# Half-height matmuls two at once, PSUM banks leased by twos, and biased logits in SBUF, in a decoder layer

## What is computed

```python
x = _layernorm(x + _L0_attn_ref(x, ...))        # scores = LN(x) K^T, 1024 keys, relu, square, times V, per head of 64
x = _layernorm(x + _L0_xattn_ref(x, ctx, ...))  # 16 heads of 16; logits + stoich_bias, softmax, times V, Wo
x = _layernorm(x + _L0_ffn_ref(x, ...))         # 256 -> 1024 -> 256 with relu, low-rank part of the top-1 expert
...
        D = jnp.clip(frac[:, None, :] - frac[:, :, None], CLAMP_MIN, CLAMP_MAX)
        stoich_bias = ap * jnp.maximum(D, 0.0)[:, None] + an * jnp.minimum(D, 0.0)[:, None]
        attn = gamma * logits + delta * stoich_bias
        probs = jax.nn.softmax(attn, axis=-1)
```

## Time and profile before

| | |
|---|---|
| median of 3 runs | 865.58 us (864.62 to 867.97) |
| profiled execution, its own time | 868.24 us |
| span of its profile | 866.4 us |
| mean granted TensorE clock | 0.987 |
| busy PE / DVE / ACT / POOL | 824.3 / 720.1 / 704.0 / 581.2 us |

### The profile page before, as it was taken

The page is one execution under the profiler, slowest core; times in us unless marked ns, Lnnn a source line. Parts: engine busy times, 40 slices in busy tenths (PEclk is TensorE's granted clock), DMA queues, the critical chain, the costliest instruction groups (busy, mean ns, idle before and its releaser), DMA issues.

```text
span 866.4 us, 23427 instructions
## 1 busy us (share of the span) xinstructions
PE 824.3 (95%) x8444; PEld 594.3 (69%) x8444; DVE 720.1 (83%) x2148; ACT 704.0 (81%) x1930; POOL 581.2 (67%) x754
## 2 busy tenths in 40 slices
PE   7889899999999999999999999999999999999896
PEld 6545556767777676767767676676768667667686
DVE  5887988887888888888888888888888887889854
ACT  3658998897888989798897979888898988888841
POOL 5677878675777868586786768678776867543511
PEclk9998999999999999999999999999999999999899
DMA  7233222222131213223122312313231321323100
GB/s 170 99 65 69 50 56 44 42 40 56 44 62 44 56 38 57 45 52 67 44 57 44 68 26 60 59 45 61 50 63 20 64 55 32 62 45 56 32 14 25
DMA packets 38149, 46.32 MB, mean 53 GB/s; under 512 B 10417, under 2 KB 27313, under 8 KB 38034
## 3 DMA queue, kind: packets, MB, share of 16 engines
q1 hardware_dynamic: 38034, 44.82, 26.0%
HBM read 15.42 MB, written 4.19 MB: 23 GB/s over the span
## 4 chain that ended last, share of the span: by engine, by line
PE 84%; DVE 5%; ACT 4%; issue 2%; POOL 2%; SPq 1%; DMA 1%; POOLq 0%; DVEq 0%; ACTq 0%
PE bank L308 12%; PE bank L503 12%; PE bank L295 11%; PE bank L256 10%; PE bank L421 8%; PE bank L435 7%; PE bank L405 4%; PE bank L381 4%; PE bank L362 2%; PE bank L328 2%; PE bank L342 2%; PE bank L513 2%; PE bank L387 2%; ACT P L711 1%; DVE T L939 1%
## 5 line engine op out<-in xcount | busy, mean ns | idle before, releaser
L1165 POOL TENSOR_TENSOR R<-R 128x512 f32<-128x512 f32 x208 | 220.4, 1063 | 74.8 <-ACT R L655 74.4
L711 ACT ACTIVATE P<-T,NM 128x256 f32<-128x256 f32 x512 | 256.9, 512 | 13.0 <-DVE NM L939 12.9
L1183 POOL TENSOR_SCALAR U<-DP,alph 128x512 f32<-128x512 f32 x256 | 188.1, 736 | 108.5 <-DVE NM L939 72.8
L930 DVE SCALAR_TENSOR_TENSOR bank<-DN,alph,bank 128x512 f32<-128x512 f32 x256 | 180.2, 749 | 47.3 <-PE bank L405 47.1
L939 DVE CUSTOM_DVE_ANT_0 T<-bank,U 128x256 f32<-128x256 f32 x512 | 185.9, 419 | 2.4 <-POOL U L1183 1.3
L655 ACT ACTIVATE R<-bank 128x512 f32<-128x512 f32 x248 | 134.0, 597 | 30.9 <-PE bank L295 29.2
L633 ACT ACTIVATE STG<-bank 128x512 f32<-128x512 f32 x256 | 138.5, 596 | 13.9 <-PE bank L421 12.5
L308 PE MATMUL bank<-R,VS 128*32 128x512 f32 x992 | 120.6, 602 | 6.2 <-DVE R L884 3.8
L295 PE MATMUL bank<-SK,KH 64*128 64x512 f32 x480 | 107.4, 443 | 5.7 <-ACT XO L655 2.4
L711 ACT ACTIVATION_READ_ACCUMULATOR P<-T,NM 128x1 f32 x512 | 103.6, 202 | 0.0
L421 PEld LDWEIGHTS bank<-ident,P 64*128 64x128 f32 x2048 | 77.1, 140 | 36.4 <-issue 27.7
(11 more groups left out here) (180 smaller groups left out, 1826.2 us busy)
## 6 DMA issues: line engine op xcount, KB each, us to landing
QS<-QK SPq DMA_DIRECT2D x384, 64.0 KB, 2.3
XG<-in_x SPq DMA_DIRECT2D x16, 256.0 KB, 3.0
CT<-in_ctxT SPq DMA_DIRECT2D x16, 256.0 KB, 2.9
out<-XO SPq DMA_DIRECT2D x15, 256.0 KB, 2.5
FK<-in_frac SPq DMA_DIRECT2D x16, 128.0 KB, 3.2
STG<-in_wiT SPq DMA_DIRECT2D x2, 512.0 KB, 5.5
STG<-in_woT SPq DMA_DIRECT2D x2, 512.0 KB, 4.3
STG<-in_kT SPq DMA_DIRECT2D x2, 256.0 KB, 4.1
```

Of the source, the lines that this page charges most:

```text
L711: eng.activation(P[n % NP][:, cs], T[n % NT][:, cs], ACT.Exp, bias=NM[:, n % 8, q:q + 1], scale=-1.0, accum_out=SU[n // 16 % 2][:, q, seat ...
L930: eng.scalar_tensor_tensor(out=L[:, :], in0=dn[:, :], scalar=alph[:, 16 + h:17 + h], in1=L[:, :], op0=ALU.mult, op1=ALU.add).then_inc(s_t1, 1)
L1165: eng.tensor_tensor(r, r, r, ALU.mult).then_inc(s_sqp, 1)
L1183: eng.tensor_scalar(U[n % NU][:, :], dp[:, :], alph[:, h:h + 1], 0.0, ALU.mult, ALU.add).then_inc(s_u, 1)
```

## The change

- Every full-height product is cut into two half-height ones (rows 0 to 63 and 64 to 127). `products` issues them in pairs: in phase 0 the lower half of product `x` beside the upper half of product `y`, in phase 1 the halves crossed. The two go to different banks. Phase 1 waits on a semaphore (`s_half`) that the last matmul of phase 0 sets, since it adds to the same banks from the other rows. `kp` and `vp` are paired with each other, the others with their own second half. The transposes are cut in the same way, and the fillers too. Only `av`, `values` and one small product (`bias_o`) keep 128 rows. The count of matmuls in the program goes from 7342 to 10488.
- PSUM: six banks are three pairs, and every step leases a pair (`lease`), picked at build time by a table of expected durations. The logits lose their own two banks and lease a pair as well. `fo` and the two `fi` of a batch hold a pair each for long.
- `biased`: the first operation writes `T` in SBUF, not the bank, and waits for `T` to be free (`s_ex`); the second reads `T` and `U`, both in SBUF. A logits pair is free after the first operation (`s_t1`), and `logits` no longer waits for `s_tt`.
- `y1` becomes two operations on half the columns; other readers of transposed tiles read two banks with a strided pattern.
- All numbers of the order tables are new (a few are shown).

```diff
-        psum = [ctx.enter_context(nc.psum_tensor(f"bank{i}", [128, 512], f32)) for i in range(8)]
-        pL, pV, pA = psum[4:6], psum[6], psum[7]
+        turf = ctx.enter_context(nc.psum_tensor("turf", [128, 6, 512], f32))
+        psum = [turf[:, k, :] for k in range(6)]
+        pV, pA = (ctx.enter_context(nc.psum_tensor(n, [128, 512], f32)) for n in ("valued", "heads"))
...
+        def quads(ap):
+            return ap.rearrange("p (a j x) -> p a j x", j=2, x=64)
+
+        def both(name, b, i=0):
+            k = place[name, b, i]
+            return turf[:, k:k + 2, :]
+
+        def woven(name, b, rows=slice(0, 128), a=4):
+            return both(name, b)[rows, :, 0:64 * a].rearrange("p j (a x) -> p a j x", x=64)
+
+        moment, expected, tenant, bank_of, place = [0], [-99999] * 3, [None, None, None], {}, {}
+        LEASE = {"lg": 21, "turn": 28, "sc": 26, "fi": 86, "fo": 197, "kp": 65, "qp": 34, "op": 22, "gate": 25,
+                 "gsT": 2, "uT": 18, "xnT": 26, "otT": 40, "x1T": 18, "rcT": 23, "x2T": 12, "bo": 452}
...
-        def take(name, b, i=0, keep=False):
-            k = ring.pop(0)
-            if not keep:
-                ring.append(k)
-            before = used.get(k)
-            used[k] = (name, b, i)
-            bank_of[name, b, i] = psum[k]
-            return psum[k], before
-
-        def give_back(name, b, i=0):
-            ring.append([k for k in used if used[k] == (name, b, i)][0])
+        def lease(*names):
+            p = min(range(3), key=lambda q: (expected[q], q))
+            expected[p] = max(expected[p], moment[0]) + LEASE[names[0][0]]
+            before, tenant[p] = tenant[p], names
+            for j, n in enumerate(names):
+                bank_of[n], place[n] = psum[2 * p + j], 2 * p + j
...
+            def two(name, b, i=0):
+                banks, before = lease((name, b, i), (name, b, i + 1))
+                banks_free(before)
+                return banks
+
+            def products(x, y, terms, phase, fresh):
+                for n, (lx, rx, ly, ry) in enumerate(terms):
+                    eng.matmul(x, lx[half(phase), :], rx[half(phase), :], start=(fresh and n == 0), stop=False,
+                               skip_group_check=True)
+                    end = eng.matmul(y, ly[half(1 - phase), :], ry[half(1 - phase), :], start=(fresh and n == 0),
+                                     stop=False, skip_group_check=True)
+                return end
 
...
-                        i = eng.transpose(bank[:, hp * 256 + t * 128:hp * 256 + t * 128 + 128],
-                                          XN[:, t, hp * 128:hp * 128 + 128], ident[:, :])
+                        for j in range(2):
+                            o = hp * 128 + t * 64
+                            i = eng.transpose(banks[j][:, o:o + 64], XN[half(j), t, hp * 128:hp * 128 + 128],
+                                              ident[half(j), half(j)])
...
+            def kp_vp(b, phase):
+                if phase == 0:
+                    _, before = lease(("kp", b, 0), ("vp", b, 0))
+                    banks_free(before)
+                    pe.wait_ge(s_wlo["k"], 1)
+                    pe.wait_ge(s_wlo["v"], 1)
+                    pe.wait_ge(s_ch, b + 1)
+                    pe.wait_ge(s_cl, b + 1)
+                else:
+                    pe.wait_ge(s_half["kp"], b + 1)
+                x, y = bank_of["kp", b, 0], bank_of["vp", b, 0]
+                (kh, kl), (vh, vl) = W["k"], W["v"]
                 for m in range(2):
                     cs = slice(m * 128, m * 128 + 128)
+                    terms = []
                     for k in range(2):
+                        terms += [(kh[:, k, cs], CH[:, k, :], CH[:, k, cs], vh[:, k, :]),
+                                  (kl[:, k, cs], CH[:, k, :], CH[:, k, cs], vl[:, k, :]),
+                                  (kh[:, k, cs], CL[:, k, :], CL[:, k, cs], vh[:, k, :])]
+                    o = slice(m * 256, m * 256 + 256)
+                    end = products(x[:, o], y[:, o], terms, phase, phase + m == 0)
+                if phase == 0:
+                    end.then_inc(s_half["kp"], 1)
+                else:
+                    end.then_inc(s_kvp, 1)
...
             def logits(p):
                 G, m = p // 2, p % 2
                 pe.wait_ge(d_q[G % 2], 96 * (G // 2 + 1))
-                pe.wait_ge(s_tt, 4 * p)
+                pL = two("lg", 0, 2 * p)
...
+            def ffn_in(b, v):
+                u, phase = v // 2, v % 2
+                if phase == 0:
+                    two("fi", b, 2 * u)
+                    pe.wait_ge(s_wlo["i0"], 1)
+                    pe.wait_ge(s_wlo["i1"], 1)
+                    pe.wait_ge(s_x2l, b + 1)
                 else:
+                    pe.wait_ge(s_half["fi"], 2 * b + u + 1)
                 for i in range(2):
+                    x, y = (bank_of["fi", b, 2 * u + j][:, i * 256:i * 256 + 256] for j in range(2))
+                    cx, cy = (slice((4 * u + 2 * j + i) * 128, (4 * u + 2 * j + i) * 128 + 128) for j in range(2))
+                    terms = []
                     for k in range(2):
+                        for w, z in ((WI[0], X2H), (WI[0], X2L), (WI[1], X2H)):
+                            terms.append((w[:, k, cx], z[:, k, :], w[:, k, cy], z[:, k, :]))
+                    end = products(x, y, terms, phase, phase + i == 0)
+                if phase == 0:
+                    end.then_inc(s_half["fi"], 1)
+
+            def low_rank(b, v):
+                u, phase = v // 2, 1 - v % 2
...
+                if piece % 2:
+                    pe.wait_ge(s_half["fo"], 2 * b + piece // 2 + 1)
+                x, y = (bank_of["fo", b, j][:, 0:256] for j in range(2))
+                pe.wait_ge(s_il, 4 * b + piece // 2 * 2 + 2)
+                terms = []
+                for c in range(piece // 2 * 4, piece // 2 * 4 + 4):
+                    tx, ty = (slice((c % 2) * 256 + t * 128, (c % 2) * 256 + t * 128 + 128) for t in range(2))
+                    for h, w in ((IH, WP[0]), (IH, WP[1]), (IL, WP[0])):
+                        terms.append((h[:, c // 2, tx], w[:, c, :], h[:, c // 2, ty], w[:, c, :]))
+                end = products(x, y, terms, int(piece in (1, 2)), piece == 0)
+                if piece % 2 == 0:
+                    end.then_inc(s_half["fo"], 1)
+                elif piece == 3:
+                    end.then_inc(s_fo, 1)
 
...
-                for b, u in due(g, -11, 8, 74, early=35, late=5):
+                for b, u in due(g, 18, 8, 70, early=-27, late=-28):
                     logits(8 * b + u)
-                for b, u in due(g, 1309, 4, 29, early=-19, late=239):
+                for b, u in due(g, 1295, 4, 23, early=-3, late=528):
                     ffn_in(b, u)
-                for b, u in due(g, 1310, 4, 29, early=-16, late=370):
+                for b, u in due(g, 1340, 4, 12, late=531):
...
-                b3 = bank_of["otT", b, 0][:, :].rearrange("p (t c) -> p t c", t=2)
+                x4 = quads(xg[:, :, :].rearrange("p t c -> p (t c)"))
                 dve.wait_ge(s_otT, b + 1)
-                eng.scalar_tensor_tensor(out=xg[:, :, :], in0=xg[:, :, :], scalar=2.0, in1=b3, op0=ALU.mult,
-                                         op1=ALU.add).then_inc(s_y1, 1)
-                dve.wait_ge(s_y1, b + 1)
+                for j in range(2):
+                    b3 = bank_of["otT", b, j][:, 0:256].rearrange("p (a x) -> p a x", x=64)
+                    eng.scalar_tensor_tensor(out=x4[:, :, j, :], in0=x4[:, :, j, :], scalar=2.0, in1=b3, op0=ALU.mult,
+                                             op1=ALU.add).then_inc(s_y1, 1)
+                dve.wait_ge(s_y1, 2 * b + 2)
                 stats("b", b, xg)
 
...
-                    h, L = head(n), pL[n % 2]
-                    eng.scalar_tensor_tensor(out=L[:, :], in0=dn[:, :], scalar=alph[:, 16 + h:17 + h],
+                    h, t, L = head(n), T[n % NT], bank_of["lg", 0, n]
+                    dve.wait_ge(s_ex, 2 * (n - NT + 1))
+                    eng.scalar_tensor_tensor(out=t[:, :], in0=dn[:, :], scalar=alph[:, 16 + h:17 + h],
                                              in1=L[:, :], op0=ALU.mult, op1=ALU.add).then_inc(s_t1, 1)
                 for n in pair:
-                    u, t, L = U[n % NU], T[n % NT], pL[n % 2]
+                    u, t = U[n % NU], T[n % NT]
                     dve.wait_ge(s_t1, n + 1)
                     dve.wait_ge(s_u, n + 1)
-                    dve.wait_ge(s_ex, 2 * (n - NT + 1))
                     for q in range(2):
                         cs = slice(q * 256, q * 256 + 256)
-                        eng.tensor_tensor_reduce(out=t[:, cs], in0=L[:, cs], in1=u[:, cs], scale=-1.0, scalar=BIG,
+                        eng.tensor_tensor_reduce(out=t[:, cs], in0=t[:, cs], in1=u[:, cs], scale=-1.0, scalar=BIG,
                                                  op0=ALU.add, op1=ALU.min,
```

(13 more changed lines are left out.)

599 lines of the change are left out of this document (265 added, 334 removed).

## The result

The changed kernel takes 901.03 us (median of 4 runs, 899.67 to 902.93) where the kernel before takes 865.32 us (4 runs on the same chip): a ratio of 1.041, 95% interval 1.038 to 1.044. It is 35.7 us slower; 16.7 was forecast. The span of its profile is 901.1 us, against 866.4.

A forecast was written before the change was run, and what follows sets the result against it. TensorE (49.5 of 50.0 us a batch) bounds the kernel before; afterwards VectorE, at 51.2. The added 1.2 us over 14 batches is +17 on 868.24: 885, less 2.7 for the median: 882 us, range 836 to 920.

The forecast's parts named there:

- the lock: VectorE bursts with two SBUF inputs and GpSimd operations take turns on shared ports, overlapping about 0.1 us: 7.3 us a batch.
- VectorE as the bound: Middle batches: VectorE busy 49.4 us, 51.2 with waits for ScalarE, against TensorE's 47.5.
- The start and the end I leave as they are.: Kernel's first and last parts, some 70 us each: no change forecast; the added 1.2 us applied to 14 steady batches.
- The wait of the bursts: VectorE's eight bursts a batch: 7.3 us added by waiting for GpSimd; bounds 4.5 and about 10.
- 1.8 us a batch of waits for `IH`: VectorE waiting for ScalarE's answers: 28.6 us in all, taken to stay whatever the period is.
- TensorE's term: TensorE's matmuls and transposes: -51 - 10 + 5 + 1 + 15 = -40 us, 2.5 us a batch.
- a second phase behind its first: TensorE drains between phases at 52 places: 0.27 to 0.3 us each, +15 us in all.
- a change of shape: TensorE switching array rows and columns in use: about 0.20 us each, 254 fewer, -51 us.
- The faster rival: TensorE stays the bound and the change pays: 48.4 us a batch, 839 us; chance 0.31.
- The banks' rival: Three PSUM pairs stall TensorE: four places, 6 us a batch, 53.5 us a batch, 918 us; chance 0.13.
- L930's -1.0 us a batch: First operation of `biased` writing SBUF: 749 ns priced at L890's 687, 16 a batch.
- 911: Time in us if GpSimd's 9.41 us inside bursts count in full, 2.1 us a batch more.

The follow-up runs named there:

- small_gp: Changed kernel with GpSimd's `U` and squares writing 32 of 512 columns, part of the computation left out: 864.1 us, ratio 0.997.
- before_small: Kernel before with GpSimd's `U` and squares cut to 32 of 512 columns, part of the computation left out: 857.8 us, ratio 0.992.
- lg_in_bank: Changed kernel with `biased` writing back to the logits' bank, the burst reading it, and the pair leased to the burst's end: 957.8 us, ratio 1.106.
- before_sbuf: Kernel before with `biased` writing `T` in SBUF, the burst reading `T` and `U` there, and the free-`T` wait moved ahead: 929.0 us, ratio 1.073.
- whole_products: Changed kernel with full-height products, one bank per phase, and no `s_half` waits between phases: 927.6 us, ratio 1.071.
- small_gp_free: `small_gp` with UL's copies reading constants so nothing waits for `uT`'s pair, more of the computation left out: 864.5 us, ratio 0.996.
- lg_late: Changed kernel, burst still reading SBUF, but the logits' pair leased until the burst's end (`s_tt`): 1027.6 us, ratio 1.186.
- guard: Changed kernel with GpSimd waiting for a burst's end ahead of 53 of its 338 two-input operations: 897.7 us, ratio 1.034.

## Why the prediction was wrong in size

The side was right, and the lock is there. The rise is twice the forecast, and what the forecast made of the lock, VectorE as the bound, did not come. By the medians, the cut of GpSimd's two operations gives the kernel before 7.7 us (865.6 to 857.8) and the changed one 37.0 (901.0 to 864.1). The difference, **29 us, is what those two operations and the bursts lose to each other** (31 if each run is taken against the kernel before of its own chip). The other **6 us** (864.1 against 857.8) are what halves, leases and places cost in sum, together with XN's gain and bias, which the bursts of `small_gp` still meet. Nearly all of the 6 is in the first three batches: 137.2 us in `small_gp`, 130.5 in `before_small`. The split takes it that the cut acts on both kernels alike. That it gives 7.2 us to `lg_in_bank`, which has no lock and no full engine, speaks for this; it is no proof.

- **The step that failed: "The start and the end I leave as they are."** I put the lock on 14 steady batches, 1.2 us each, since the view I had read closely was that of the middle. Its 11 steady batches did take 1.25 us more each, 13.8 in all. But the stretches that I had left at nothing gave 20.9 us of the 34.7, the first three batches 15.5 of them. `before_sbuf`, which has nothing of the change but the SBUF inputs, shows the start's share by itself: its first three batches take 149.4 us, at a mean clock of 0.97, against 135.5 before and 151.0 after. `small_gp` brings them to 137.2. The lower clock adds to the start of the changed kernel; by the distances of `whole_products` it is some 5 of the 15.5 us there, an estimate (TensorE is busy at the lower level for 21.4 us of this stretch after, for 9.5 before). First `before_sbuf`, then `small_gp`, then `before_small`:

```profile
62.70:212.10 149.40, 126.88 (x1324) 82.67 (x1325) 133.82 (x357) 121.04 (x343) 116.12 (x132) 0.97 0.24 46
57.70:194.90 137.20, 123.17 (x1680) 82.58 (x1682) 115.00 (x360) 120.39 (x344) 60.90 (x130) 0.95 0.28 53
57.40:187.90 130.50, 123.25 (x1336) 82.08 (x1335) 109.70 (x359) 121.00 (x346) 51.25 (x131) 1.00 0.28 53
```

- **The wait of the bursts was sized at 7.3 us a batch; it is 3.5** (55.6 us over 16), below my lower bound of 4.5. I counted every microsecond of GpSimd inside a burst as one in which the burst can't run. Most of it is `U`, which the burst's own second operation releases, and which then waits itself: 963 ns on average for the first head's `U`, 723 for the second's. Of the bursts' 55.6 us `U` caused 0.6, squares 29.0 and XN's two operations 21.1.
- **VectorE as the bound, 49.4 us busy and 51.2 with its waits, fell.** It is busy for 46.3 of 51.5. The 1.8 us a batch of waits for `IH`, which I had taken to stay whatever the period is, went from 28.6 to 10.7 us in all. That the period came out within 0.3 us is no credit to the sum: its errors met. No engine is full, and the chain passes through all four, 43, 25, 14 and 6%.
- **TensorE's term was too large.** 2.5 us a batch were to be saved; it is 1.5 (546.1 to 529.4 over eleven), and a batch has TensorE busy for 48.0 us where 49.5 less 2.5 would be 47.0. The 256-column pair starts every 0.12 us, the full one's price, as forecast. But the entry cost is not gone: the first pair after transposes still takes 0.08 us more (385.69, 385.89, then 386.02), where I forecast nothing. And a second phase behind its first costs 0.34 us, not 0.27 to 0.3: from the last pair of the first phase to the second pair of the second it is 0.57 us where two steps of 0.12 would do. The 0.26 us of the waits above (13.3 us for 52) is only what the load of the weights waited. With 0.34 and 0.12 in the sum, both this saving and the shapes' 1.6 us a batch of `whole_products` come to 0.13 to 0.14 us for a change of shape, an estimate, where I had 0.20.

```profile
385.69 0.36 PE L277 MATMUL turf<-Woh,CH 64*128 64x256 f32 x1
385.89 0.28 PE L277 MATMUL turf<-Wol,CH 64*128 64x256 f32 x1
386.02 0.28 PE L277 MATMUL turf<-Woh,CL 64*128 64x256 f32 x1
...
386.37 0.28 PE L277 MATMUL turf<-Woh,CL 64*128 64x256 f32 x1
386.71 0.38 PE L277 MATMUL turf<-Woh,CH 64*128 64x256 f32 x1
386.94 0.28 PE L277 MATMUL turf<-Wol,CH 64*128 64x256 f32 x1
```

- **What TensorE did save bought next to nothing.** The eleven middle batches take 547.1 us in `small_gp` and 550.3 in `before_small`, most of them 50.0 in both. Against the changed kernel, though, `whole_products` lost 27.2 us in its eleven batches where it added 29.7 to TensorE's. So TensorE's time counts when it grows, and where it shrank other waits took the saving.
- **The faster rival's condition was met, and it did not come.** It was to decide "if the burst's added wait is under some 4 us a batch"; the wait is 3.5. `before_sbuf` shows why this did not help: the loss of VectorE reaches TensorE through the waits between them, whatever idle time VectorE has elsewhere. (Nor does its 48.4 us a batch follow from the terms given: 51.2 less half of 7.3 is 47.6.)
- **The banks' rival (0.13) was partly right.** A middle batch of `small_gp` has ten waits for a pair, and taking away the longest moved it to the next (`small_gp_free`). These waits are the likely reason why the saving is kept back, but XN's meetings with the burst are still there in both runs, and no run parts the two. The rival's price of four places at 1.5 us was too high, and its mechanism, readers behind a burst, is that of `lg_late`. I had named the early release as a point against it; it is worth 127 us.
- **L930's -1.0 us a batch was wrong.** I priced the output to SBUF by L890; L937 takes 740 ns where L930 took 749, -0.15 a batch.
- By the Trainium skill's rule ("SBUF — State Buffer", "Who interferes with whom") I had worked out 911. That one of the two fully blocks holds here in both directions, as the timeline above shows. Who is served next is another matter: `U` starts at 380.46 behind the burst operation of 380.29, and the one of 380.63 still goes ahead of it. Both sums, mine and the one by the rule, counted waits that fall on GpSimd as VectorE's.

What stays open: why the lock costs 29 us in the changed kernel when `guard`, with two thirds of the bursts' waits gone (55.6 to 19 us), gives back 3.3. That GpSimd's waits count as much as VectorE's fits all runs, but no run removes the lock and leaves GpSimd's work and the early release in place.

## What to carry to other kernels

Read the stages in which the bound engine of the middle is not the bound, before calling a cost hidden, and ask which engine waits for the one that gets slower: `before_sbuf` lost 63 us where VectorE had 7 us of idle time in each batch. A shared resource costs only one of two engines at each meeting; find out from the trace which, before giving all of it to one. Price the release of a buffer apart from the operation that ends it: here holding a pair of banks to the end of the burst costs more than anything that the matmuls' shape gives. And before a busy time confirms a price, look at the clock beside it: in `whole_products` two fifths of what seemed to be the shapes' cost was the lower clock.

## What the runs showed of the hardware

- Which engine waits goes by GpSimd's kind of operation. I took the GpSimd operations of 512 columns that start inside one burst operation and 0.13 to 0.27 us ahead of the next. A TENSOR_TENSOR (squares, XN, X1b) went first in 41 of 41 cases of the changed kernel, and the next burst operation waited it out. A TENSOR_SCALAR (`U`), at 0.16 to 0.24 us, went first in none of 84 and waited itself. 380.46 against 380.63 is one of these. In `lg_late` it is 44 of 44 and 0 of 94.
- A burst operation that had waited ended 0.27 to 0.29 us after GpSimd's, in all cases of the changed kernel.
- A second phase right behind its first costs TensorE 0.34 us (mean of 36 of the changed kernel's, 0.32 to 0.36).
- From half-height transposes to half-height products the entry costs 0.08 us (0.20 to the second pair's start instead of 0.12). From half-height products to `scores` and `logits` nothing is lost: the next start comes after 0.11 us, where after a full-height matmul of the kernel before it came after 0.21.
- At the lower of its two clock levels a 256-column matmul started every 0.21 us instead of 0.12 (`whole_products`).
